# A MoE layer with linear-bias attention: the shared expert's half chunk, low parts in the free rows of its high parts' tile

## The reference

```python
x = L0_attn_x
xn = _layernorm(x, axis=-1)
x = x + _L0_attn_ref(xn, L0_attn_W_kqv) + _L0_ffn_ref(xn, ...)

def _swiglu_mlp(x, wg, wu, wd):
    return jax.nn.silu(x @ wg) * (x @ wu) @ wd
...
return y + _swiglu_mlp(identity, sw_gate, sw_up, sw_down)   # sw_down: 704 x 256
```

## Time and profile before

| | us |
|---|---|
| median of 3 runs | 2511.07 |
| lowest and highest of them | 2509.58, 2511.92 |
| the profiled execution, its own time | 2507.22 |
| span of its trace | 2505.4 |
| busy in the span: PE, DVE, ACT, POOL | 2393.8, 1912.8, 1559.5, 779.8 |
| mean granted TensorE clock | 0.975 |

### The profile page before, as it was taken

The page is one execution under the profiler, slowest core; times in us unless marked ns, Lnnn a source line. Parts: engine busy times, 40 slices in busy tenths (PEclk is TensorE's granted clock), DMA queues, the critical chain, the costliest instruction groups (busy, mean ns, idle before and its releaser), DMA issues.

```text
span 2505.4 us, 53355 instructions
## 1 busy us (share of the span) xinstructions
PE 2393.8 (96%) x19286; PEld 1475.1 (59%) x19286; DVE 1912.8 (76%) x2905; ACT 1559.5 (62%) x3210; POOL 779.8 (31%) x901
## 2 busy tenths in 40 slices
PE   6999999994999999947999999999999999999998
PEld 5888888884999999942333333333333333333333
DVE  5666666656555555549999999999999999999994
ACT  3333333334333333312888888888888888888888
POOL 2222222224222222240113333333333333333333
PEclk9999999996999999976999999999999999999999
DMA  6999877771222222235252534353535343525321
GB/s 186 181 160 175 170 131 143 138 118 32 74 76 73 77 74 76 71 61 93 49 83 59 95 61 95 61 95 61 95 61 95 62 96 61 95 62 96 62 61 42
DMA packets 177923, 229.03 MB, mean 91 GB/s; under 512 B 42828, under 2 KB 127436, under 8 KB 177656
## 3 DMA queue, kind: packets, MB, share of 16 engines
q1 hardware_dynamic: 153048, 172.02, 36.3%
q0 software_dynamic: 22448, 50.56, 8.5%
q10 hardware_dynamic: 2176, 3.02, 0.3%
HBM read 131.47 MB, written 93.66 MB: 90 GB/s over the span
## 4 chain that ended last, share of the span: by engine, by line
PE 52%; DVE 1%; DMA 1%; SPq 0%; ACT 0%; issue 0%; POOLq 0%; POOL 0%
PE p_o L1349 23%; PE p L1339 19%; PE p L1326 8%; PE p L1359 1%; DVE part L1177 1%; PE p L1332 1%; DMA q_op<-m_row 0%; DMA k_op<-ali_scratch 0%; POOLq L1078 0%; POOL q_op L1077 0%; SPq L1026 0%; ACT probs L1301 0%; SPq L1013 0%; ACT o_sb L1289 0%; SPq L1039 0%
## 5 line engine op out<-in xcount | busy, mean ns | idle before, releaser
L1177 DVE TENSOR_REDUCE part<-p 128x2 f32<-128x1024 f32 x1024 | 1243.2, 1221 | 89.9 <-PE p L1326 82.6
L1301 ACT ACTIVATE probs<-p 128x512 f32<-128x512 f32 x2048 | 1112.7, 597 | 162.8 <-PE p L1339 137.4
L1326 PE MATMUL p<-k_op,q_op 50*128 50x512 f32 x2048 | 759.2, 461 | 43.3 <-DMA k_op<-ali_scratch 32.3
L1339 PE MATMUL p<-q_op,k_op 51*128 51x512 f32 x2048 | 757.8, 452 | 1.2 <-DMA q_op<-m_row 0.4
L1349 PE MATMUL p_o<-probs,v_op 128*32 128x256 f32 x8192 | 655.0, 391 | 4.4 <-ACT o_sb L1289 0.8
L1339 PEld LDWEIGHTS p<-q_op,k_op 51*128 51x128 f32 x2048 | 310.7, 185 | 418.2 <-ACT probs L1301 374.5
L1349 PEld LDWEIGHTS p_o<-probs,v_op 128*32 128x32 f32 x8192 | 163.0, 108 | 359.4 <-ACT probs L1301 306.3
L1326 PEld LDWEIGHTS p<-k_op,q_op 50*128 50x128 f32 x2048 | 303.8, 188 | 58.6 <-issue 32.5
L1105 POOL TENSOR_TENSOR att<-o_t,rec 128x256 f32<-128x256 f32 x63 | 39.0, 618 | 825.4 <-DVE rec L1195 825.4
L751 POOL DMA_INDIRECT xe<-xn_scratch,ids x135 | 143.5, 1063 | 370.7 <-DMA ids<-lists_scratch 368.5
L830 ACT ACTIVATE gated_e<-p_gate 128x352 f32<-128x352 f32 x135 | 62.6, 464 | 192.6 <-PE p_gate L771 192.6
(11 more groups left out here) (173 smaller groups left out, 4044.4 us busy)
## 6 DMA issues: line engine op xcount, KB each, us to landing
qk_scratch<-qk_out SPq DMA_DIRECT2D x64, 512.0 KB, 12.7
k_op<-qk_scratch SPq DMA_DIRECT2D x192, 128.0 KB
q_op<-qk_scratch SPq DMA_DIRECT2D x192, 128.0 KB
yr_scratch<-y SPq DMA_DIRECT2D x135, 128.0 KB, 1.7
v_scratch<-v_out SPq DMA_DIRECT2D x16, 1024.0 KB, 13.2
v_op<-v_scratch SPq DMA_DIRECT2D x32, 512.0 KB, 10.0
x<-in_x SPq DMA_DIRECT2D x16, 512.0 KB, 4.3
xn_scratch<-xn SPq DMA_DIRECT2D x16, 512.0 KB
```

The lines of the kernel that those rows point to most:

```text
L1177: v.tensor_reduce(part[c_ % 2][:, kh, :, qb], p1[use % 2][:], AX.X, ALU.max, negate=True).then_inc(s["s1_read"], 1)
L1301: a.activation(probs[kb % 4][:, h], p2[use % 3][:], ACT.Exp).then_inc(s["s2_read"], 1)
L1326: return t.matmul(p1[use % 2][:, x], q_op[u][lo:lo + S1_ROWS, pair, q0:q0 + P], k_op[u][lo:lo + S1_ROWS, pair, kh * 512:(kh + 1) * 512], s ...
L1339: t.matmul(p2[use % 3][:], k_op[u][lo:lo + S2_ROWS, pair, kb * P:(kb + 1) * P], q_op[u][lo:lo + S2_ROWS, pair, half * HQ:(half + 1) * HQ], ...
```

## The change

For the half chunk alone, VectorE writes the low parts not to `h_lo` rows 64 to 127 but to `h_hi` rows 0 to 63, the rows that the high parts leave free. TensorE then takes the whole 128 rows of `h_hi` times the whole 128 rows of the high weights, which is low by high plus high by high, and rows 64 to 127 of `h_hi` times the low weights. Each token block has two products in place of three: one of 128 rows and one of 64 rows. The five full chunks compute what they did.

```diff
-                rows = slice(SL, P) if ch == SC - 1 else slice(0, P)
-                v.tensor_tensor(h_lo[j % HR][rows], h_sb[j % 2][rows], h_hi[j % HR][rows].bitcast(F32),
-                                ALU.subtract).then_inc(s["h_lo_ok"], 1)
+                if ch == SC - 1:
+                    v.tensor_tensor(h_hi[j % HR][0:SL], h_sb[j % 2][SL:P], h_hi[j % HR][SL:P].bitcast(F32),
+                                    ALU.subtract).then_inc(s["h_lo_ok"], 1)
+                else:
+                    v.tensor_tensor(h_lo[j % HR][:], h_sb[j % 2][:], h_hi[j % HR][:].bitcast(F32),
+                                    ALU.subtract).then_inc(s["h_lo_ok"], 1)
...
-                rows = slice(SL, P) if ch == SC - 1 else slice(0, P)
                 for b in range(TB):
                     cols = slice(b * P, (b + 1) * P)
+                    if ch == SC - 1:
+                        t.matmul(p_y[:, b], h_hi[j % HR][:, cols], s_dn[0][:, ch],
+                                 start=False, stop=False, skip_group_check=True)
+                        last = t.matmul(p_y[:, b], h_hi[j % HR][SL:P, cols], s_dn[1][SL:P, ch],
+                                        start=False, stop=True, skip_group_check=True)
+                        continue
                     for i, (hh, dd) in enumerate(((h_hi, 0), (h_hi, 1), (h_lo, 0))):
-                        last = t.matmul(p_y[:, b], hh[j % HR][rows, cols], s_dn[dd][rows, ch],
-                                        start=(ch == 0 and i == 0 and b % 2 == 0), stop=(ch == SC - 1 and i == 2),
+                        last = t.matmul(p_y[:, b], hh[j % HR][:, cols], s_dn[dd][:, ch],
+                                        start=(ch == 0 and i == 0 and b % 2 == 0), stop=False,
                                         skip_group_check=True)
                 last.then_inc(s["dn_ps"], 1)
```

## The result

| us | before | after |
|---|---|---|
| median | 2510.01 (5 runs, 2507.89 to 2511.92) | 2523.93 (5 runs, 2521.95 to 2530.6) |
| the profiled execution's own time | 2507.22 | 2528.71 |
| span of its trace | 2505.4 | 2526.9 |
| mean granted clock | 0.975 | 0.973 |

What follows compares the result with a forecast made beforehand. TensorE's instruction stream was taken to bound `front`. Fifteen half chunks at +0.71 us (+10.7 us) and +1.0 us at the stage's end gave +11.7 us on 2511.1, so 2522.8 us; range 2514 to 2530 us.

Steps and rivals of the forecast that it cites:

- What bounds the kernel: In `front`, TensorE's instruction stream sets the pace, 34.086 us per tile, and nothing covers time added or removed.
- Products removed: In the half chunk, four products and their weight loads fewer per tile, 0.117 us each, 0.47 us less.
- Price of a change of form: In the half chunk, each change between 128 and 64 rows costs 0.20 us; six more per tile add 1.20 us.
- Sum per tile: In `front`, added changes of form less removed products, taken as +0.71 us for each of 15 half chunks, +10.7 us.
- Stage's end: The last half chunk of `front`, at the lower clock of 1.2 GHz, takes 3.85 us in place of 2.83, +1.0 us.
- VectorE's write: VectorE's half-chunk subtraction, now writing to other partitions than it reads, costs 0; bounds 0 and 0.7 us per tile, hidden.
- Total: Whole kernel: 10.7 + 1.0 = +11.7 us, median 2522.8 us, +0.47%.
- The first (a price of the edges): Half chunk: the 0.20 us belongs to entering and leaving it, alternation inside is free; 7.9 us less, 2503.2 us; chance 0.08.
- the second (one part paid): Half chunk: only drain or load is paid per change, 0.10 us; +2.5 us, 2513.6 us; chance 0.07.
- The third, that alternation lowers the clock: `front`: the granted clock falls, or each change costs 0.31 us; about +22 us, 2533 us; chance 0.05.

Runs made afterwards that it cites:

- full-rows kernel: Changed kernel with the second product of each half-chunk block also on all 128 rows; 2502.7 us beside 2513.9 before, ratio 0.9956.
- the increments: Changed kernel plus 128 increments of an unused semaphore on TensorE at the start of the experts' block; 2525.0 us beside 2514.5 before, ratio 1.0040.
- twelve products on 128 rows: Kernel before with all twelve half-chunk products on 128 rows, rows 0 to 63 holding old values; 2507.8 us beside 2513.6 before, ratio 0.9973.

## Why the prediction was right

**What bounds the kernel.** That `front` goes at TensorE's pace and nothing covers it held: a change of the half chunk's length came back in the period one to one, in both directions. VectorE did not become the bound even at 33.2 us a tile: between 40 and 580 us TensorE of the full-rows kernel waits for it once, 7.0 us in the last tile, as in before. One reading was loose: the clock row hides that in the first tile the granted clock is 0.50 from 33.8 to 37.0 us; every kernel here has such a stretch, and it bears on no term of the sum.

**Products removed.** 0.117 us each was expected. (34.087 - 33.614) / 4 = 0.118 at two changes, (33.707 - 33.233) / 4 = 0.119 at none.

**Price of a change of form.** The 0.20 us came from a single seam on each side, against the earlier trace rows. The runs give it from differences in which nothing else varies. With eight products, the periods at 0, 2, 4 and 8 changes are 33.233, 33.614, 34.020 and 34.793: 0.190, 0.197 and 0.195 us per change. With twelve, at 0, 2 and 8 they are 33.707, 34.087 and 35.247: 0.190 and 0.193. One price of 0.193 us fits all seven kernels within 0.02 us a tile, whichever product or edge the change stands at. The statement of the Trainium skill, TensorEngine Tiling (Array Packing), under Key Properties, that a change of tiling mode drains TensorE, fits what is seen: 0.09 to 0.10 us before each load (202.70 to 202.91, where 0.12 is plain). The other half of the price, the load that nothing hides, is in the weight loads' own rows. That the first half is such a drain is read from the page; the runs show its length and place.

Every product of 64 rows here uses rows 64 to 127, so the runs do not tell the number of rows from their place. Nor is every change of the number a change of form that costs: in `experts` of before the products go from 128 to 96 rows at the plain pace of 0.12 us.

```profile
701.06 0.28 PE L790 MATMUL pe_y<-wdn_hi,ht_lo 128*128 x1
701.17 0.28 PE L790 MATMUL pe_y<-wdn_hi,ht_hi 96*128 x1
701.29 0.28 PE L790 MATMUL pe_y<-wdn_lo,ht_hi 96*128 x1
```

**Sum per tile.** +0.71 us expected, +0.706 measured. **Stage's end.** +1.0 us expected, VectorE's wait grew by 0.93 (3.78 to 4.71). **VectorE's write.** Nothing expected, 687 ns against 689. **Total.** `front` +11.7 us expected, 11.6 in the first pair of profiles, 12.1 and 11.9 between the later ones, and 11.5 in all three pairs when it is counted from the first product of `values`. The median's 2523.9 us is 1.1 us above the predicted 2522.8. That agreement is in part luck: the changed kernel gave 1.0052 and 1.0067, and 1.0040 with the increments, 10 to 17 us, and the predicted 1.0047 lies just outside the interval of the second. The sum explains the edited stage; 2 to 4 us of the medians of both measurements lie outside it.

**The rivals.** The first (a price of the edges) is excluded by the twelve products on 128 rows and by 34.793 us in place of 33.6, and the second (one part paid) by the 0.31 us between products. The third, that alternation lowers the clock, was given 0.05 and held against by the attention's clock. The fall did not occur in `front` in the profiles of the changed kernel, but it exists: with twelve products the clock fell twice, right behind a half chunk. That argument from the attention was too strong. Whether it happens in some unprofiled execution of the changed kernel is open.

**What was missed.** The prediction said that the stages behind `front` would have their old lengths. The second profile is 21.5 us longer, of which 9.9 are those stages. Their scatter, 1924 to 1938 us over 14 profiles, was not in the sum or named as a source of error, though it is as large as the effect.

## What to carry to other kernels

Count the changes of row form on TensorE, not only the products: in this kernel one change between 128 and 64 rows costs 0.19 to 0.20 us, as much as 1.6 products of 256 columns, so a shorter list in a worse order is slower. When a product of 64 rows stands in a stream of 128-row products, order them in groups, or better fill the free rows with something that is right or harmless, since a product of 64 rows is no cheaper than one of 128. When an effect of 0.5% is measured, compare the stage that was edited and its period across profiles; the rest of the kernel moves by as much on its own.

## What the runs showed of the hardware that was not expected

The granted clock fell to its lower level inside a stage in which the profile shows TensorE busy without a gap, twice right behind a half chunk of twelve products with eight changes of form, at a cost of 1.5 us each. The return of the clock at the attention's start came 24 us later in one execution of the same kernel than in another (68 us behind the first product in place of 44), which is worth 10 us. In `experts` a wait of TensorE of 1.6 or 2.1 us for gathered rows had such a fall behind it, and the two together made most of the difference between a stage of 492.5 and one of 499.0 us. And some tiles of that stage, 7 apart, last 0.5 to 1.3 us longer; which ones they are follows the number of TensorE instructions ahead of them. A version in which 64-row products on the two halves of the rows run side by side was not tried.
